# Attention over sorted edges: the multiply that carries the running sums on, placed on GpSimd instead of VectorE, and the mask copy of a group split in two

## What is computed

```python
w_m = (efeat @ W_msg + b_msg).reshape(E, in_f, -1)
w_a = (efeat @ W_attn + b_attn).reshape(E, in_f, -1)
h_src = feat[src][:, :, None]
e1 = w_m * h_src
e2 = w_a * h_src
seg_max = jax.ops.segment_max(e2, dst, num_segments=N)
ex = jnp.exp(e2 - seg_max[dst])
denom = jax.ops.segment_sum(ex, dst, num_segments=N)
attn = ex / denom[dst]
ft = jax.ops.segment_sum(e1 * attn, dst, num_segments=N)
return ft.sum(axis=1)
```

## Time and profile before

| what | value |
|---|---|
| three runs | 9868.96, 9891.31, 9896.46 us, median 9891.31 |
| profiled execution | 9850.59 us, its span 9848.8 us |
| busy share of the span: TensorE, VectorE, GpSimd, ScalarE | 72%, 70%, 54%, 19% |
| data moved | 747.17 MB, 76 GB/s on average |
| mean granted TensorE clock over the span | 0.856 of full speed |

### The profile page before, as it was taken

The page is one execution under the profiler, slowest core; times in us unless marked ns, Lnnn a source line. Parts: engine busy times, 40 slices in busy tenths (PEclk is TensorE's granted clock), DMA queues, the critical chain, the costliest instruction groups (busy, mean ns, idle before and its releaser), DMA issues.

```text
span 9848.8 us, 230469 instructions
## 1 busy us (share of the span) xinstructions
PE 7140.4 (72%) x89519; PEld 6577.9 (67%) x89519; DVE 6910.7 (70%) x13614; ACT 1829.5 (19%) x4253; POOL 5359.1 (54%) x5017
## 2 busy tenths in 40 slices
PE   5888865777777776667776358888588887588884
PEld 5777755666666666666666347877477777577774
DVE  6666657888888888888888656666456655455563
ACT  0000003444444444444444300000000000000000
POOL 3555555555555555555555545555455554555554
PEclk9999987777777777777778679999799999799997
DMA  2222213343444443443334311111111111111110
GB/s 78 68 70 70 67 36 91 122 123 123 122 122 123 122 122 122 122 122 122 122 122 122 104 49 39 40 38 38 25 38 41 38 38 32 29 37 38 38 38 21
DMA packets 809009, 747.17 MB, mean 76 GB/s; under 512 B 217377, under 2 KB 769121, under 8 KB 808897
## 3 DMA queue, kind: packets, MB, share of 16 engines
q1 hardware_dynamic: 649088, 653.49, 20.3%
q0 software_dynamic: 154864, 90.47, 6.0%
q10 hardware_dynamic: 5008, 2.59, 0.1%
HBM read 229.59 MB, written 519.73 MB: 76 GB/s over the span
## 4 chain that ended last, share of the span: by engine, by line
PE 59%; issue 17%; DVE 17%; POOL 3%; ACT 3%; DMA 1%; DVEq 1%; ACTq 0%; SPq 0%; POOLq 0%
PE ps L756 43%; PE ps L806 9%; PE ps L799 6%; DVE amax_room L1129 4%; DVE flat L1161 3%; DVE spare L1134 2%; DVE ps L870 2%; DVE flat L870 2%; POOL got L439 2%; DVE stt L870 1%; ACT wide_buf L670 1%; ACT ps L671 1%; POOL wide_buf L439 1%; ACT aring L676 1%; POOL flat L439 0%
## 5 line engine op out<-in xcount | busy, mean ns | idle before, releaser
L439 POOL DMA_INDIRECT msg<-feat,cidx x2016 | 1986.6, 985 | 1871.7 <-PE ps L756 788.1
L756 PE MATMUL ps<-parts,wide_buf 128*128 128x112 bf16 x37632 | 2142.4, 218 | 641.9 <-issue 362.9
L756 PEld LDWEIGHTS ps<-parts,wide_buf 128*128 128x128 bf16 x37632 | 1985.6, 101 | 792.1 <-issue 783.1
L756 PE MATMUL ps<-parts,flat 128*128 128x112 bf16 x37632 | 2171.8, 219 | 431.6 <-issue 420.8
L439 POOL DMA_INDIRECT hsrc<-feat,aidx x1568 | 1535.8, 979 | 1635.4 <-DMA aidx<-src_sorted 1248.0
L756 PEld LDWEIGHTS ps<-parts,flat 128*128 128x128 bf16 x37632 | 2002.5, 101 | 586.7 <-issue 577.5
L806 PE MATMUL ps<-wsb,zT 102*128 102x192 f32 (+1 forms) x9408 | 2039.9, 371 | 8.7 <-ACT zT L664 8.6
L799 PE MATMUL ps<-idm,z_room 128*102 128x128 f32 x4704 | 1119.4, 363 | 1275.5 <-DVE flat L870 1031.6
L806 PEld LDWEIGHTS ps<-wsb,zT 102*128 102x128 f32 x9408 | 1956.5, 243 | 16.0 <-ACT zT L664 11.2
L870 DVE TENSOR_TENSOR raw<-ps,amask 128x1792 f32<-128x1792 f32 x224 | 453.5, 2025 | 1773.2 <-remote 958.5
L799 PEld LDWEIGHTS ps<-idm,z_room 128*102 128x102 f32 x4704 | 680.9, 169 | 1519.3 <-issue 668.3
(11 more groups left out here) (210 smaller groups left out, 4265.5 us busy)
## 6 DMA issues: line engine op xcount, KB each, us to landing
state_tab<-flat SPq DMA_DIRECT2D x784, 512.0 KB
raw<-quot_tab SPq DMA_DIRECT2D x224, 512.0 KB
run_tab<-run SPq DMA_DIRECT2D x224, 224.0 KB
top_tab<-spare SPq DMA_DIRECT2D x392, 128.0 KB
msg<-feat,cidx POOLq DMA_INDIRECT x2016
hsrc<-feat,aidx POOLq DMA_INDIRECT x1568
efs<-in_ef SPq DMA_DIRECT2D x392, 34.0 KB, 1.9
msg<-in_x,cidx POOLq DMA_INDIRECT x672
```

Of the source, the lines that this page charges most:

```text
L439: return pool.indirect_dma_start(dest, None, table, rows_at(idx))
L756: last = nc.tensor.matmul(slot[s][:, t, 0:QW].rearrange("p (q c) -> p q c", c=D), hot[s][:, m, t * P:(t + 1) * P], parts[:, m * Q:(m + 1) ...
```

## The change

`rescaled` leaves VectorE's step and becomes an instruction of GpSimd, issued behind the outer product of the group two later; VectorE's first running sum waits for it by a new semaphore. The one mask copy of ScalarE becomes two: the masks of the maxima go ahead of the group's transpose copies, those of the sums behind the second half of the exponentials, with a semaphore of their own.

```diff
 # GpSimd
+                def rescaled(j, s):
+                    pool.wait_ge(a_gap[s], j + 1)
+                    pool.wait_ge(a_exp[s], (j + 1) * NEXP)
+                    nc.gpsimd.tensor_tensor(stt[:], st[:, 1 - s, G - 1, :].rearrange("p (t c) -> p t c", t=2),
+                                            egap.unsqueeze(1).to_broadcast([P, 2, DD]), ALU.mult).then_inc(a_resc[s], 1)
...
                     for s in range(2):
                         outer(j, s, False)
+                        rescaled(j - 1, s)
                         fetch(j + 1, s, False)
                 for s in range(2):
                     outer(AHALF - 1, s, False)
+                    rescaled(AHALF - 2, s)
+                for s in range(2):
+                    rescaled(AHALF - 1, s)
 # ScalarE
-            def masks(j, s):
-                nc.scalar.activation(aring[:, s], resets[:, :, bass.ds((2 * j + s) * G, G)], ACT.Copy).then_inc(a_ring[s], 1)
+            def maxima_mask(j, s):
+                nc.scalar.activation(aring[:, s, 0], neg[:, bass.ds((2 * j + s) * G, G)], ACT.Copy).then_inc(a_ring[s], 1)
+
+            def sums_mask(j, s):
+                nc.scalar.activation(aring[:, s, 1], keep[:, bass.ds((2 * j + s) * G, G)], ACT.Copy).then_inc(a_keep[s], 1)
 
             def group(j, s):
                 b, jb = 1 - s, j - 1 + s
+                maxima_mask(j, s)
                 for k in range(G):
                     if k == G - 1:
                         weights(jb, b, 0)
                     turned(j, s, k)
-                masks(j, s)
                 weights(jb, b, 1)
+                sums_mask(j, s)
 # VectorE
-                def rescaled(j, s):
-                    dve.wait_ge(a_exp[s], j * NEXP + 3)
-                    return mark(tt(stt[:], st[:, 1 - s, G - 1, 0:2 * DD].rearrange("p (t c) -> p t c", t=2),
-                                   egap.unsqueeze(1).to_broadcast([P, 2, DD]), ALU.mult))
...
                     m = running_max(s, 2)
-                    if again:
-                        dve.wait_ge(a_sum[s], j * G)
-                    r = rescaled(jb, b)
                     need(m)
                     m = running_max(s, 3)
                     if put_before:
                         dve.wait_ge(a_put[b], 32 * jb)
                     dve.wait_ge(a_w[b], 2 * jb + 2)
-                    need(r)
+                    dve.wait_ge(a_resc[b], jb + 1)
                     running_sum(jb, b, 0)
+                    dve.wait_ge(a_keep[b], jb + 1)
```

More of the change, by code:

```diff
@@ L293, in gnn_program @@
         a_gap = ring("a_gap")
+        a_resc = ring("a_resc")
         a_ring = ring("a_ring")
+        a_keep = ring("a_keep")
         a_put = ring("a_put")
@@ L683, in group @@
                     turned(j, s, k)
-                masks(j, s)
                 weights(jb, b, 1)
+                sums_mask(j, s)
+            maxima_mask(0, 0)
             for k in range(G):
                 turned(0, 0, k)
-            masks(0, 0)
+            sums_mask(0, 0)
             group(0, 1)
@@ L1163, in running_sum, with step @@
                     out.then_inc(a_sum[s], 1)
-                def step(j, s, again, put_before):
+                def step(j, s, put_before):
                     b, jb = 1 - s, j - 1 + s
@@ L1215, in attention @@
                 dve.wait_ge(a_d[0], 2)
-                step(0, 1, False, False)
-                step(1, 0, True, False)
+                step(0, 1, False)
+                step(1, 0, False)
                 with dve.Fori(1, AHALF - 1) as j:
                     loop_start()
-                    step(j, 1, True, True)
-                    step(j + 1, 0, True, True)
+                    step(j, 1, True)
+                    step(j + 1, 0, True)
                 loop_start()
-                step(AHALF - 1, 1, True, True)
+                step(AHALF - 1, 1, True)
                 loop_start()
@@ L1226, in attention @@
                     weighted(AHALF - 1, 1, piece)
-                need(rescaled(AHALF - 1, 1))
+                dve.wait_ge(a_resc[1], AHALF)
                 dve.wait_ge(a_put[1], 32 * (AHALF - 1))
                 dve.wait_ge(a_w[1], 2 * AHALF)
+                dve.wait_ge(a_keep[1], AHALF)
                 for k in range(G):
```

## The result

| | median | range | runs |
|---|---|---|---|
| before | 9891.31 us | 9856.16 to 9912.47 | 5 |
| changed | 9807.35 us | 9784.56 to 9816.41 | 5 |

The ratio is 0.9929, with a 95% interval of 0.9908 to 0.9949: 70 us faster (50 to 91). The medians alone lie 84 us apart. The forecast was 190 us faster. The time lies inside the range of 9,600 to 9,860, but the gain is less than half of what was forecast, so the sum had a term wrong.

A forecast was written before the change was run, and what follows sets the result against it. Chains, not one full engine, bound the kernel: two attention loops at 10.24 us a step. 10.24 - 0.46 (rescaling) - 0.08 (masks) + 0.05 (lateness) = 9.75, saving 0.49 x 392 = 192 us: 9,700 us, range 9,600 to 9,860.

The forecast's parts named there:

- The two loops: In attention, VectorE-TensorE-ScalarE-VectorE and GpSimd with SyncE's queue both run at the step's pace, 10.24 us.
- The masks: VectorE's 0.61 us wait a step mostly hides a wait for the exponential; splitting the copy saves 0.08 us a step.
- The rescaling off VectorE: Max 2 to max 3 falls from 0.99 to 0.53 us, saving VectorE 0.46 us a step.
- The price of the product: The rescaling multiply on GpSimd takes 1.05 us, scaled from the outer product's 2.07 us for 1088 elements.
- Can the second loop follow?: GpSimd's loop shortens to 9.73 us as its index wait falls to 2.77, meeting the first loop at about 9.75.
- an index wait that stays above 3: Sign in the profile after that the forecast is wrong: GpSimd's wait for indices, expected to fall from 3.17 to about 2.8 us.
- as VectorE gets ahead of GpSimd: States are written earlier relative to the outer product, so GpSimd's index wait shortens, to 2.77 us.
- It isn't delayed: The fetch behind the moved instruction on GpSimd: its 1.05 us fits into the index wait of 2.77 to 3.26 us.
- GpSimd's loop doesn't follow: Rival, 15%: the index wait stays near 3.17 us, the step stops at 10.13, time 9,850 us.
- The handoff costs more than it saves: Rival, 7%: at the first running sum's new wait, a 2.07 us operation lengthens such steps by 0.46 us; up to 10,070 us.
- The clock takes it back: Rival, 10%: TensorE meets half speed more often, the 10.24 us step stays, time 9,890 us.
- theory G: Theory set up after the result: GpSimd's own loop of outer product, index wait and gathers holds the step.

The follow-up runs named there:

- before_idx_early: The kernel before with the source indices loaded a step earlier, not behind the outer product: 8527.43 us, ratio to before 0.9996.
- idx_early: The changed kernel with the source indices loaded a step earlier, not behind the outer product: 8241.27 us, ratio to before 0.9657; again on another chip 9698.89 us, 0.9838.
- no_rescale: The changed kernel without the rescaling multiply and its wait, the first running sum adding zeros: 8348.4 us, ratio to before 0.9785.
- bare_idx_early: The changed kernel with no rescaling anywhere and the source indices loaded a step earlier: 9484.92 us, ratio to before 0.9614.
- half_rescale: The changed kernel with GpSimd multiplying only 256 of the 512 elements, the other half left as zeros: 9717.56 us, ratio to before 0.9853.
- the exponential: The changed kernel with the gap's exponential moved ahead of the fourth transpose copy on ScalarE: 8398.67 us, ratio to before 0.9876.
- masks_only: The kernel before with only the mask copy split, the rescaling staying on VectorE: 8531.0 us, ratio to before 0.9998.
- both_early: The changed kernel with source indices loaded and the gap's exponential taken early: 8151.81 us, ratio to before 0.9553; again (_2) on another chip 9463.9 us, 0.9601.

## Why the prediction was right or wrong

**The two loops: right in kind.** That GpSimd's loop has hardly any slack (10.13 of 10.24 us; the 10.22 also holds the idle time ahead of the outer product, and would be the step whatever sets it), that the list of waits hides this, and that it would have to follow if the first loop got shorter, was the right thing to look at. `before_idx_early` shows that it didn't bind before, `idx_early` that it binds after.

**The masks: right against the wait list, wrong by a little as a term.** Of 0.61 us waited, none was to be had by the split alone (the forecast took 0.08 a step). In the changed kernel it is worth 0.13 us a step; why isn't shown.

**The rescaling off VectorE: right about max 2 and max 3.** Their starts moved from 0.99 us apart to 0.51 (medians of the stage), where 0.53 was forecast. The sum of 9.75 us for the first loop isn't confirmed by the 9.77 of `no_rescale`; that they agree is luck. GpSimd's loop set that step, as forecast with 2.77 of waiting, while the first loop alone can do 9.26 (`bare_idx_early`). The forecast left TensorE's part as it was, but TensorE's busy time per step fell from 7.19 to 6.61 us at a granted clock of 0.86.

**The price of the product: too low.** I took 1.05 us, scaled from the outer product of 2.07 us for 1088 elements, "as the two instructions are of one kind". It takes 1.27. The Trainium skill, GPSIMD Engine Reference, section Performance versus the Vector engine, had the better number: its 1.96 times of VectorE's 0.69 makes an estimate of 1.35; the rows after give 1.266 / 0.697 = 1.82. The outer product was the wrong neighbour: by the line of the two measured sizes 1088 elements would take 2.5 us (an estimate). That both its inputs are broadcast may be the reason; no run tests it. In the typical step (the median) the first running sum starts 0.63 us behind max 3 instead of 0.39, about the 0.22 by which the price was too low. On average VectorE idles 0.32 us a step there, 0.27 above the 0.05 allowed. But the price alone isn't what the step hangs on: that wait is also 0.29 in `half_rescale`, with a product of 0.73 us.

**The step that failed is "Can the second loop follow?": the wait for indices was to shrink from 3.17 to 2.77 us, so that both loops met at 9.75.** From the outer product's end to the first gather the changed kernel takes 3.03 us. GpSimd's loop is then 2.08 + 3.03 + 3.87 + 0.99 (between the gathers) = 9.97 us, where the sum had 9.73. The step is 10.0. These 0.24 us times 392 are 94 us of what is missing. The forecast itself named an index wait that stays above 3 as a sign that it is wrong.

The dependence that the forecast used is there: indices asked for later behind the states' transfers come sooner. What it had wrong is "as VectorE gets ahead of GpSimd". VectorE's first running sum now waits for a product that stands in GpSimd's queue behind the outer product, so VectorE can't get ahead as it was meant to. The distance from states to request went from 3.17 to 3.35 us only, and the forecast needed 5.9; without the product it is 5.72, and the wait 2.77. That it is this tie which holds the distance back fits all five rows of the table; no run takes away the tie and leaves all else.

"It isn't delayed", said of the fetch, was wrong too, but it matters less. The product was checked against the index wait by its length alone: 1.05 us fits into 2.77. But GpSimd runs in order, and an instruction costs its own wait too, here 0.64 us a step and in single steps 2.05. In 41 of 300 steps the gathers were held by it, at 3.46 us behind the outer product; in the other 259 they came 2.96 us behind it, held by the indices.

Then the loops feed each other: a late outer product makes the product late, that delays the first running sum, and its step, and later the index load behind the states. This is why repairing one of the two gave only part (the exponential: 8 us beyond the changed kernel, on another chip; the indices: 165 and 101 us) and both together gave 254 us more than the changed kernel on one chip and 336 on another. The coupling is shown by these runs; the share of each part in a single number isn't, as the parts don't add up.

**The rivals.** The one given 15%, "GpSimd's loop doesn't follow", with 9,850 us, is what happened, in a milder form: 9,807 us and a wait of 3.03 instead of 3.17. Its reason was another, more transfers in a shorter step, and not VectorE held back by the product; and the 40% of the earlier trace rows are all transfers, the gathers too, not SyncE's alone. "The handoff costs more than it saves" had the right place, with a price in between (1.27 + 0.17 for the handoffs in the step shown, against its deciding 1.83). "The clock takes it back" may be seen in `masks_only`, and otherwise only its opposite: as the step gets shorter, the granted clock rises, 0.80 before, 0.81 after, 0.86 with both early loads. In the kernel before each of the 219 falls of the clock from 2000 to 5000 us comes between 0.9 us ahead of and 2.3 us behind the end of TensorE's idle time before the transposes (not every idle time has one: the 2.73 us of the earlier trace rows are not followed by a fall, the next 2.80 us are). That idle time is 2.65 us on average before, 2.52 after and 2.10 in `both_early_2`, so it got shorter, as the forecast had argued. So part of what the last kernels gain may be clock, and 9.30 us lies below the 9.70 that the forecast's own terms (0.46 and 0.08) would make.

What stays open is why the changed kernel gains 56, 70 and 125 us on three chips. The time from outer product to first gather moves with it, 3.12, 3.03 and 2.97 us on average, as theory G would have it, but three points don't show which is cause.

The version that beats both kernels is `both_early`: ratio to before 0.9553 and 0.9601 on two chips, and 254 to 336 us below the changed kernel.

## What to carry to other kernels

When an instruction moves to another engine, ask four things of its new queue: its price there, with the uncertainty that a dissimilar neighbour leaves; how long it will itself stand and wait; what stands behind it; and whether it ties two engines together that had been free to drift apart. Here the last was the costly one. An engine whose loop is nearly full isn't free because it is idle half the time: 54% busy here, with a closed loop through a DMA of 10.13 us in a step of 10.24. If two loops are within a few per cent of each other, an edit on one may show little until the other is shortened too, so try the repairs together before dropping either: here one showed 8 us alone, across two chips, and 89 us behind the other. Busy time plus idle time makes the step on every engine; only removing a wait, as `before_idx_early` and `idx_early` do, tells whether its loop binds.

## What the runs showed of the hardware

- A multiply of two f32 inputs on GpSimd took 0.726 us for 256 and 1.266 for 512 elements a partition, while one with both inputs broadcast took only 2.07 us for 1088.
- A load of indices behind 1 MB of transfers on the same queue was used sooner the later it was asked for: 3.17 us from outer product to gather at a distance of 3.17 us, 2.77 at 5.72.
- The step of 10.24 us stays with either small edit (`masks_only`, `before_idx_early`), each on another chip than the profile of the kernel before; the granted clock of the stage was 0.78 and 0.79 there, 0.80 before.
- The same program took 8,531 us on some chips and 9,855 us and more on others: the difference lies outside attention, about 4,530 against 5,820 to 5,890 us, and wasn't followed up.
